# Grouped attention in a gated cross-attention and mixture-of-experts block: TensorE's order changed to one maximum, exponentials, the other maximum, half a chunk's values, with fewer products on constants

## The chip, the cores and the metric

One core of a Trainium2 chip runs the whole program. The time is device microseconds (us) for one execution. The engines are TensorE (PE, with its weight loads PEld), VectorE (DVE), ScalarE (ACT), GpSimd (POOL) and SyncE (SP), which here issues DMAs.

## The reference

```python
q = (Q @ w_q.T).reshape(B, S, G, HG, HD)      # G = 8 groups, HG = 4 heads, HD = 16
k = (K @ w_k.T).reshape(B, S, G, HD)
v = (V @ w_v.T).reshape(B, S, G, HD)
scores = jnp.einsum('bnghd,bmgd->bnghm', q, k) / scale
scores = jnp.where(causal, scores, NEG_INF)
attn = jax.nn.softmax(scores, axis=-1)
out = jnp.einsum('bnghm,bmgd->bnghd', attn, v).reshape(B, S, D)
return out @ w_o.T + b_o
```

Four batches of 512 tokens, width 512. The attention above takes a layernorm of x as its queries; its result, times tanh of a gate, is added to x. A mixture of experts follows (16 experts, 4 per token, and a shared one), again gated and added. The change lies in the attention alone.

## The kernel before

Stages run one after the other: projections of q, k and v to DRAM (`stage_project`), attention (`stage_attend`), output projection and router logits (`stage_close`), routing, experts, combination. `stage_attend` is written by hand for each engine, with semaphores; no scheduler moves anything.

It makes 32 iterations (NIT), one for each batch and group, over 4 heads and 512 x 512 scores. Keys are cut in 4 chunks of 128 (CH). The scores are computed twice. The first time, TensorE multiplies 128 queries by the keys (`max_unit`, L445, into the banks a_mb0 and a_mb1), and VectorE takes the maximum of each row (L413). The maxima are transposed (`turn_maxima`, L451) and put by DMA as one more row beside q. The second time, two iterations later (AHEAD = 2), TensorE computes the transposed scores less their maximum (`exp_unit`, L465, into a_eb), ScalarE takes the exponential into a_at (L392), GpSimd clears the part above the diagonal (L334), and TensorE multiplies by the values (`pv_unit`, L476, into a_pv). ScalarE copies a_pv out once in an iteration (L383).

A chunk `ch` of an iteration has two units `j`, of two heads `t` each. The head t = 0 has its q and k in partitions 0 to 48, t = 1 in partitions 64 to 112, so the two products of a pair use different halves of the array's rows. Chunk `ch` of the exponentials has 512, 384, 256 and 256 columns; the maxima that are computed beside it, for the iteration two later, have 512, 384, 256 and 256 columns too. The values of a chunk have 512, 384, 256 and 128 columns, and four heads stand beside each other in the array's columns.

TensorE's queue in an iteration is, for each chunk: unit j = 0 (exponentials of two heads, maxima of two heads), unit j = 1 (the same), then the values of the chunk before it, all four heads in full width. Waits in this queue:

```python
                    if not isinstance(i, int) or u >= 2:
                        eng.wait_ge(s_rmax, u)
```

is the wait of each maximum u for VectorE to have read the same bank, two maxima before; `exp_unit` waits for ScalarE to have read its bank, a chunk before; `pv_unit` waits for GpSimd (`s_causal`), and at chunk 0 also for ScalarE's copy of a_pv (`s_o`).

Ahead of the exponentials of each unit `spin` issues products of two constant matrices (bf16, 128 x 128, L456) into the bank that the exponentials then overwrite. FILL = (12, 6, 2, 0) is their number in a unit of chunk 0 to 3, so 40 in an iteration; in iteration 0 it is 24 in every unit. Nobody reads their results. Iterations 1 to 29 have maxima beside them, 30 and 31 have none.

Of the kernel before, what the change touches and what calls it, by code (L numbers as in the profile page):

```python
# [16 lines left out]
P = 128  # L17
BATCH, SEQ, D = 4, 512, 512
T = BATCH * SEQ
KD = D // P  # L20
GROUPS, HG, HD = 8, 4, 16
CH = SEQ // P
NIT = BATCH * GROUPS
VW = 2 * HD
HALF = 64
ROW_PAD, ROW_MAX = 3 * HD, 3 * HD + 1
NB = 4
# [241 lines left out]

def stage_attend(nc, io, dram):  # L270

    AHEAD, SPIN, FILL = 2, 96, (12, 6, 2, 0)
    with ExitStack() as c:
        sb = lambda n, s, d=F32: c.enter_context(nc.sbuf_tensor(n, s, d))
        ps = lambda n, s: c.enter_context(nc.psum_tensor(n, s, F32))
# [3 lines left out]
        def sem(name):  # L279
            sems.append(dsem(name))  # L280
            return sems[-1]

        q, k = io["q"], io["k"]
        v = [sb(f"a_v{i}", [P, CH, VW]) for i in range(NB)]
        at = [sb(f"a_at{i}", [P, CH, HG, SEQ]) for i in range(2)]
# [3 lines left out]
        mb = [ps(f"a_mb{i}", [P, SEQ]) for i in range(2)]  # L289
        eb = [ps(f"a_eb{i}", [P, 2, SEQ]) for i in range(2)]  # L290
        pv, mt = ps("a_pv", [P, SEQ]), ps("a_mt", [HG * CH, P])
        s_out = dsem("a_sout")
        s_ld = [dsem(f"a_sld{i}") for i in range(NB)]
        s_smax, s_rmax, s_mt, s_mr = (sem(f"a_s{n}") for n in ("smax", "rmax", "mt", "mr"))
        s_row = [dsem(f"a_srow{i}") for i in range(NB)]
        s_sexp, s_exp, s_causal, s_pv, s_o, s_kept = (sem(f"a_s{n}") for n in ("sexp", "exp", "causal", "pv", "o", "kept"))
# [5 lines left out]
        def steps(eng, body):  # L302

            for r in range(NB):
                body(r, r, 0)
            with eng.Fori(1, NIT // NB - 1) as t:
                for r in range(NB):
                    body(t * NB + r, r, t)
            for r in range(NB):
                body(NIT - NB + r, r, NIT // NB - 1)  # L310

        def after(i, first):

            return not isinstance(i, int) or i >= first

        def exists(i):
            return not isinstance(i, int) or i < NIT

        @block.gpsimd
        def _(eng):  # L320

            due = eng.alloc_register("due7")
            eng.reg_mov(due, NB * 2 * CH + 2)

            def body(i, r, t):
                for ch in range(CH):
                    for hp in range(2):
                        if isinstance(i, int):
                            eng.wait_ge(s_exp, i * 2 * CH + 2 * ch + hp + 2)
                        else:  # L330
                            eng.wait_ge(s_exp, eng.snap(due))
                            eng.reg_add(due, due, 1)
                        square = at[r % 2][:, ch, 2 * hp:2 * hp + 2, ch * P:(ch + 1) * P]
                        eng.affine_select(out=square, in_=square, compare_op=ALU.is_ge, fill=0.0, base=0,  # L334
                                          pattern=[[0, 2], [1, P]], channel_multiplier=-1).then_inc(s_causal, 1)
            steps(eng, body)
# [96 lines left out]

        @block.tensor
        def _(eng):
            def max_unit(i, r, turn, j):

                ch = CH - 1 - turn
                w = max(256, (ch + 1) * P)
                for t in range(2):  # L440
                    u = i * CH * HG + turn * HG + 2 * j + t
                    if not isinstance(i, int) or u >= 2:
                        eng.wait_ge(s_rmax, u)
                    rows = slice(HALF * t, HALF * t + ROW_MAX)
                    eng.matmul(mb[t][:, 0:w], q[r][rows, j, ch * P:(ch + 1) * P], k[r][rows, 0:w], start=True, stop=True).then_inc(s_smax, 1)  # L445

            def turn_maxima(i, r):
                eng.wait_ge(s_rmax, (i + 1) * CH * HG + 1)
                if not isinstance(i, int) or i >= 1:
                    eng.wait_ge(s_mr, i + 1)  # L450
                eng.transpose(mt[:], mx[r % 2][:].rearrange("p h c -> p (h c)"), io["ident"]).then_inc(s_mt, 1)  # L451

            def spin(bank, n):

                for _ in range(n):
                    eng.matmul(bank[:, 0:P], io["onesb"], io["before"], start=True, stop=True)  # L456

            def exp_unit(i, r, ch, j):

                n0 = min(ch * P, 256)  # L460
                eng.wait_ge(s_exp, i * 2 * CH + 2 * ch + j)
                spin(eb[j][:, 0], FILL[ch] if after(i, 1) else 2 * FILL[0])
                for t in range(2):
                    rows = slice(HALF * t, HALF * t + ROW_MAX + 1)
                    mm = eng.matmul(eb[j][:, t, n0:SEQ], k[r][rows, ch * P:(ch + 1) * P], q[r][rows, j, n0:SEQ], start=True, stop=True)  # L465
                mm.then_inc(s_sexp, 1)

            def pv_unit(i, r, ch):

                eng.wait_ge(s_causal, i * 2 * CH + 2 * ch + 3)  # L470
                if ch == 0:
                    eng.wait_ge(s_o, i + 1)
                for j in range(2):
                    for t in range(2):
                        h = head(t, j)
                        mm = eng.matmul(pv[32 * h:32 * h + 32, ch * P:SEQ], v[r][:, ch, :], at[r % 2][:, ch, 2 * j + t, ch * P:SEQ],  # L476
                                        start=ch == 0, stop=ch == CH - 1, skip_group_check=True, tile_position=(0, 32 * h))
                if ch == CH - 1:
                    mm.then_inc(s_pv, 1)

            spin(pv, SPIN)
            for i in range(AHEAD):
                eng.wait_ge(s_ld[i], LD)
                for turn in range(CH):
                    for j in range(2):
                        max_unit(i, i, turn, j)
                        spin(pv, 4 * (CH - turn))
                turn_maxima(i, i)

            def body(i, r, t):  # L490
                eng.wait_ge(s_row[r], ROWS * (t + 1))
                if exists(i + AHEAD):
                    eng.wait_ge(s_ld[(r + AHEAD) % NB], LD * (t + (r + AHEAD) // NB + 1))
                for ch in range(CH):
                    for j in range(2):
                        exp_unit(i, r, ch, j)
                        if exists(i + AHEAD):
                            max_unit(i + AHEAD, (r + AHEAD) % NB, ch, j)
                    if ch:
                        pv_unit(i, r, ch - 1)  # L500
                    elif after(i, 1):
                        pv_unit(i - 1, (r - 1) % NB, CH - 1)
                        if exists(i + 1):
                            turn_maxima(i + 1, r + 1)
            steps(eng, body)
            pv_unit(NIT - 1, NB - 1, CH - 1)


def stage_close(nc, io, dram):
# [927 lines left out]
```

## Time and profile before

| | us |
|---|---|
| runs | 1811.64, 1794.19, 1826.40 |
| median | 1811.64 |
| profiled execution, its own time | 1800.01 |
| its span, first to last instruction | 1798.0 |
| mean granted TensorE clock of the span | 0.858 |
| TensorE matmul busy in the span | 1473.3 (82%) |

[...]

### The profile page before, as it was taken

The page shows a single profiled execution, that of the slowest core. Times are in us where ns is not written, and L with a number is a line of the kernel's source. Part 1 is how long each engine was busy: PE and PEld are TensorE (multiplying, and loading weights), DVE is VectorE, ACT ScalarE, POOL GpSimd, SP SyncE. Part 2 cuts the span into 40 slices and gives each one's busy share as a digit, 9 for nine tenths or more (in the row PEclk, how much of TensorE's full clock was granted, in tenths as well). Part 3 has the DMA queues.
Part 4 walks back from the last instruction along what each step waited for, and adds up shares of the span by engine and source line. Part 5 has one row for each costly group of instructions (what it writes and reads, how often), then busy time and mean ns, then how long its engine had stood idle before and what let it go on. Part 6 is the DMA issues. An engine that isn't in the chain of part 4 may idle for free. (4 is left out here: it accounts for less than half of the span.)

```text
span 1798.0 us, 29246 instructions
## 1 busy us (share of the span) xinstructions
PE 1473.3 (82%) x8596; PEld 1068.5 (59%) x8597; DVE 752.6 (42%) x1939; ACT 537.8 (30%) x951; POOL 610.9 (34%) x810
## 2 busy tenths in 40 slices
PE   6545299999999994856349999999989987799997
PEld 4222265445455452434349999898878976665674
DVE  3111066665555551335860342442443550344353
ACT  2111024444333443011004555454434533100100
POOL 4111012222211221001016777676656774131131
PEclk9778599999776977866559999999989999897997
DMA  5443312232221213544033434434434431342342
GB/s 179 136 124 113 109 34 72 68 79 62 62 62 52 72 48 93 179 185 163 1 120 114 129 130 134 150 130 139 139 112 150 166 122 57 113 134 75 117 140 70
DMA packets 100466, 194.99 MB, mean 108 GB/s; under 512 B 27492, under 2 KB 29028, under 8 KB 99400
## 3 DMA queue, kind: packets, MB, share of 16 engines
q1 hardware_dynamic: 71848, 118.35, 20.6%
q0 software_dynamic: 17200, 55.38, 10.4%
q10 hardware_dynamic: 11376, 20.71, 3.0%
q8 instruction: 24, 0.39, 0.1%
q14 instruction: 18, 0.15, 0.0%
HBM read 130.07 MB, written 64.03 MB: 108 GB/s over the span
## 5 line engine op out<-in xcount | busy, mean ns | idle before, releaser
L413 DVE CUSTOM_DVE_ANT_0 a_mb<-a_mb,late 128x256 f32<-128x256 f32 (+3 forms) x512 | 244.6, 508 | 232.2 <-PE a_mb L445 227.4
L392 ACT ACTIVATE a_at<-a_eb 128x1024 f32<-128x1024 f32 (+3 forms) x256 | 176.9, 703 | 278.8 <-PE a_eb L465 277.2
L334 POOL TENSOR_SCALAR_AFFINE_SELECT a_at<-a_at 128x256 f32<-128x256 f32 x256 | 102.7, 406 | 440.8 <-ACT a_at L392 440.4
L1028 DVE CAST e_w<-e_w 128x480 fp32r<-128x480 f32 x144 | 95.5, 672 | 321.0 <-DMA e_w<-in_w2T 321.0
L1165 PE MATMUL e_gate<-e_w,e_xT 128*128 x948 | 178.8, 340 | 40.0 <-DVE e_w L1036 36.0
L1165 PEld LDWEIGHTS e_gate<-e_w,e_xT 128*128 128x128 f32 x948 | 166.4, 201 | 51.3 <-issue 41.2
L1184 PE MATMUL e_yps<-e_w,e_hT 128*128 x711 | 185.5, 404 | 1.9 <-ACT e_hT L1097 1.4
L1165 PE MATMUL e_up<-e_w,e_xT 128*128 x948 | 174.9, 334 | 0.0
L445 PE MATMUL a_mb<-a_k,a_q 49*128 49x256 f32 (+2 forms) x512 | 149.5, 404 | 22.3 <-DVE a_mx L413 18.0
L1165 PEld LDWEIGHTS e_up<-e_w,e_xT 128*128 128x128 f32 x948 | 154.3, 193 | 0.0
L1184 PEld LDWEIGHTS e_yps<-e_w,e_hT 128*128 128x128 f32 x711 | 128.2, 189 | 27.2 <-issue 1.6
L456 PEld LDWEIGHTS a_eb<-before,onesb 128*128 128x128 bf16 x1432 | 97.3, 108 | 78.2 <-issue 66.0
L456 PE MATMUL a_eb<-before,onesb 128*128 128x128 bf16 x1432 | 131.0, 242 | 0.0
L1032 DVE TENSOR_TENSOR e_w<-e_w 128x480 fp32r<-128x480 f32 x128 | 120.5, 941 | 0.0
L1064 POOL TENSOR_TENSOR e_hT<-e_hc,e_hT 128x384 fp32r<-128x384 f32 x79 | 85.5, 1082 | 102.0 <-ACT e_hc L1098 101.2
L445 PEld LDWEIGHTS a_mb<-a_k,a_q 49*128 49x128 f32 x512 | 79.4, 209 | 66.9 <-DVE a_mx L413 61.3
L1368 PE MATMUL s_yps<-ws,s_h 128*128 128x512 f32 (+1 forms) x288 | 108.3, 515 | 10.9 <-DVE s_h L1319 8.3
L1055 POOL DMA_INDIRECT e_x<-dx,e_idx x79 | 95.1, 1204 | 62.5 <-POOL e_idx L1052 62.5
L465 PE MATMUL a_eb<-a_q,a_k 50*128 50x256 f32 (+2 forms) x512 | 115.8, 455 | 0.0
L1060 POOL TENSOR_TENSOR e_xT<-e_xc,e_xT 128x512 fp32r<-128x512 f32 x79 | 109.3, 1384 | 8.2 <-ACT e_xc L1093 2.4
L476 PE MATMUL a_pv<-a_at,a_v 128*32 128x512 f32 (+3 forms) x1024 | 108.8, 501 | 0.6 <-POOL a_at L334 0.6
L673 PE MATMUL c_op<-c_wo,c_on 128*128 128x512 f32 x128 | 63.5, 659 | 47.8 <-DVE c_on L621 30.0
(194 smaller groups left out, 1873.8 us busy)
## 6 DMA issues: line engine op xcount, KB each, us to landing
e_w<-in_w13T SPq DMA_DIRECT2D x16, 1408.0 KB
dy<-e_y ACTq DMA_DIRECT2D x79, 256.0 KB
dq<-p_parts SPq DMA_DIRECT2D x48, 256.0 KB
a_q<-dq SPq DMA_DIRECT2D x64, 192.0 KB
do<-a_o SPq DMA_DIRECT2D x32, 256.0 KB, 2.2
dx<-c_x POOLq DMA_DIRECT2D x8, 1024.0 KB, 8.2
e_w<-in_w2T SPq DMA_DIRECT2D x16, 512.0 KB
a_k<-dk SPq DMA_DIRECT2D x64, 98.0 KB
```

The costliest lines, as they stand in the source:

```text
L334: eng.affine_select(out=square, in_=square, compare_op=ALU.is_ge, fill=0.0, base=0, pattern=[[0, 2], [1, P]], channel_multiplier=-1).then_ ...
L392: eng.activation(at[r % 2][:, ch, 2 * hp:2 * hp + 2, ch * P:SEQ], eb[hp][:, :, ch * P:SEQ], ACT.Exp, scale=0.25).then_inc(s_exp, 1)
L413: eng.tensor_tensor_reduce(out=mb[t][:, 0:w], in0=mb[t][:, 0:w], in1=io["late"][:, SEQ - w:SEQ], scale=1.0, scalar=3 * NEG, op0=ALU.add, o ...
L445: eng.matmul(mb[t][:, 0:w], q[r][rows, j, ch * P:(ch + 1) * P], k[r][rows, 0:w], start=True, stop=True).then_inc(s_smax, 1)
L456: eng.matmul(bank[:, 0:P], io["onesb"], io["before"], start=True, stop=True)
L465: mm = eng.matmul(eb[j][:, t, n0:SEQ], k[r][rows, ch * P:(ch + 1) * P], q[r][rows, j, n0:SEQ], start=True, stop=True)
L476: mm = eng.matmul(pv[32 * h:32 * h + 32, ch * P:SEQ], v[r][:, ch, :], at[r % 2][:, ch, 2 * j + t, ch * P:SEQ], start=ch == 0, stop=ch == C ...
L1032: eng.tensor_tensor(w[rows, r, 1, cols], w[rows, r, 1, cols].bitcast(F32), w[rows, r, 0, cols].bitcast(F32), ALU.subtract).then_inc(s_low, 1)
L1060: eng.tensor_tensor(xT[r][:, 1], xc[:], xT[r][:, 0].bitcast(F32), ALU.subtract).then_inc(s_xlow, 1)
L1165: mm = eng.matmul(out[r][:], xT[r][:, mine, k, :], w[:, bass.ds(buf, 1), its, at:at + INTER].rearrange("p b n -> p (b n)"), start=not (min ...
L1184: mm = eng.matmul(yps[:], hT[r][0:size, mine, n, :], w[0:size, bass.ds(buf, 1), its, at:at + D].rearrange("p b n -> p (b n)"), start=not ( ...
L1368: mm = eng.matmul(yps[j % 2][:], h[0:size, mine, n, j * P:(j + 1) * P], w2[0:size, its, n, :], start=not (mine or its or n), stop=mine == ...
```

## The change

In `exp_unit` and the table FILL, the products on constants go from (12, 6, 2, 0) to (6, 3, 0, 0) for each unit, 40 to 18 in an iteration. Iteration 0 keeps its 24. `max_unit` issues one head's maximum instead of two. In the loop, head 0's maximum now stands ahead of the unit's constants and exponentials, and head 1's behind them. `pv_unit` makes half of a chunk's columns, for all four heads, and stands behind each unit instead of behind each two, so the first half of a chunk's values is asked for one unit earlier. No DMA, and nothing on the other four engines' queues, is changed.

```diff
-    AHEAD, SPIN, FILL = 2, 96, (12, 6, 2, 0)
+    AHEAD, SPIN, FILL = 2, 96, (6, 3, 0, 0)
...
-            def max_unit(i, r, turn, j):
+            def max_unit(i, r, turn, j, t):
...
-                spin(eb[j][:, 0], FILL[ch] if after(i, 1) else 2 * FILL[0])
+                spin(eb[j][:, 0], FILL[ch] if after(i, 1) else 4 * FILL[0])
...
-            def pv_unit(i, r, ch):
+            def pv_unit(i, r, ch, part):
 
-                eng.wait_ge(s_causal, i * 2 * CH + 2 * ch + 3)
-                if ch == 0:
-                    eng.wait_ge(s_o, i + 1)
+                w = (SEQ - ch * P) // 2
+                cols = slice(ch * P + part * w, ch * P + (part + 1) * w)
+                if part == 0:
+                    eng.wait_ge(s_causal, i * 2 * CH + 2 * ch + 3)
+                    if ch == 0:
+                        eng.wait_ge(s_o, i + 1)
...
                 for ch in range(CH):
                     for j in range(2):
+                        if exists(i + AHEAD):
+                            max_unit(i + AHEAD, (r + AHEAD) % NB, ch, j, 0)
                         exp_unit(i, r, ch, j)
                         if exists(i + AHEAD):
-                            max_unit(i + AHEAD, (r + AHEAD) % NB, ch, j)
-                    if ch:
-                        pv_unit(i, r, ch - 1)
-                    elif after(i, 1):
-                        pv_unit(i - 1, (r - 1) % NB, CH - 1)
-                        if exists(i + 1):
-                            turn_maxima(i + 1, r + 1)
+                            max_unit(i + AHEAD, (r + AHEAD) % NB, ch, j, 1)
+                        if ch:
+                            pv_unit(i, r, ch - 1, j)
+                        elif after(i, 1):
+                            pv_unit(i - 1, (r - 1) % NB, CH - 1, j)
+                            if j == 0 and exists(i + 1):
+                                turn_maxima(i + 1, r + 1)
```

TensorE's queue in iteration 1, chunk 1, unit 1 and chunk 2, unit 0, before (a_mb0 and a_mb1 are the two heads' banks for maxima, a_eb0 and a_eb1 the banks of the two units' exponentials, a_pv the values):

```order
L456 MATMUL a_eb1<-before,onesb 128x128 x6
L465 MATMUL a_eb1<-a_q1,a_k1 128x384 x2
L445 MATMUL a_mb0<-a_k3,a_q3 128x384
L445 MATMUL a_mb1<-a_k3,a_q3 128x384
L476 MATMUL a_pv<-a_at1,a_v1 32x512 x4
L456 MATMUL a_eb0<-before,onesb 128x128 x2
L465 MATMUL a_eb0<-a_q1,a_k1 128x256 x2
L445 MATMUL a_mb0<-a_k3,a_q3 128x256
L445 MATMUL a_mb1<-a_k3,a_q3 128x256
```

The same place in the changed kernel:

```order
L444 MATMUL a_mb0<-a_k3,a_q3 128x384
L455 MATMUL a_eb1<-before,onesb 128x128 x3
L464 MATMUL a_eb1<-a_q1,a_k1 128x384 x2
L444 MATMUL a_mb1<-a_k3,a_q3 128x384
L478 MATMUL a_pv<-a_at1,a_v1 32x256 x4
L444 MATMUL a_mb0<-a_k3,a_q3 128x256
L464 MATMUL a_eb0<-a_q1,a_k1 128x256 x2
L444 MATMUL a_mb1<-a_k3,a_q3 128x256
L478 MATMUL a_pv<-a_at1,a_v1 32x192 x4
```

The two maxima of a pair no longer stand side by side, the six constants are three and the two are gone, and the 512 columns of values are two times 256, with the exponentials of the next unit between.

TensorE's queue at the change of iteration in the changed kernel, from the last unit of iteration 1 to the first of iteration 2:

```order
L444 MATMUL a_mb0<-a_k3,a_q3 128x256
L464 MATMUL a_eb1<-a_q1,a_k1 128x256 x2
L444 MATMUL a_mb1<-a_k3,a_q3 128x256
L478 MATMUL a_pv<-a_at1,a_v1 32x128 x4
L444 MATMUL a_mb0<-a_k0,a_q0 128x512
L455 MATMUL a_eb0<-before,onesb 128x128 x6
L464 MATMUL a_eb0<-a_q2,a_k2 128x512 x2
L444 MATMUL a_mb1<-a_k0,a_q0 128x512
L478 MATMUL a_pv<-a_at1,a_v1 32x64 x4
L450 MATMUL a_mt<-ident,a_mx1 16x128
```

Before, 12 constants stood in each of the two units of chunk 0, with only exponentials and a pair of maxima between them:

```order
L456 MATMUL a_eb0<-before,onesb 128x128 x12
L465 MATMUL a_eb0<-a_q2,a_k2 128x512 x2
L445 MATMUL a_mb0<-a_k0,a_q0 128x512
L445 MATMUL a_mb1<-a_k0,a_q0 128x512
L456 MATMUL a_eb1<-before,onesb 128x128 x12
```

The longest run of constants is 6 now, and a half of the values and a lone maximum lie between two runs.

## Rows read from the trace of the kernel before

**Rows 1.** The page: span, and TensorE's granted clock in 40 slices of the span.
```profile
span 1798.0 us, 29246 instructions
...
PEclk9778599999776977866559999999989999897997
```

**Rows 2.** Windows (stretch, length, busy us and instructions of each engine, clock, DMA): iterations 1 to 29, the tail, one iteration at each clock level.
```profile
core 0: us, PE busy (x) PEld busy (x) DVE busy (x) ACT busy (x) POOL busy (x), PEclk, DMA share, GB/s
...
265.88:680.22 414.34, 392.45 (x3045) 208.21 (x3041) 237.27 (x951) 176.63 (x262) 93.01 (x232) 0.85 0.24 64
680.22:698.00 17.78, 14.39 (x153) 6.95 (x149) 0.28 (x1) 10.81 (x18) 6.06 (x16) 1.00 0.13 46
...
411.04:424.01 12.97, 12.07 (x109) 6.35 (x106) 8.27 (x34) 6.12 (x9) 3.20 (x8) 1.00 0.29 72
...
514.76:532.92 18.16, 17.79 (x110) 9.43 (x107) 8.32 (x34) 6.10 (x10) 3.25 (x8) 0.55 0.19 51
```

**Rows 3.** Waits from 240 to 690 us: total, times, longest.
```profile
PEld a_mb L445 <- DVE a_mx L413: 59.3, 159, 0.7
```

**Rows 4.** Timeline of TensorE's matmuls at clock 1.00: start, length, line, instructions [idle before].
```profile
412.14 0.51 PE L456 MATMUL a_eb<-before,onesb 128*128 128x128 bf16 x6
412.58 0.44 PE L465 MATMUL a_eb<-a_q,a_k 50*128 50x384 f32 x2
...
413.94 1.07 PE L476 MATMUL a_pv<-a_at,a_v 128*32 128x512 f32 x8
414.94 0.28 PE L456 MATMUL a_eb<-before,onesb 128*128 128x128 bf16 x2
...
421.20 0.40 PE L445 MATMUL a_mb<-a_k,a_q 49*128 49x512 f32 x2
421.53 0.84 PE L456 MATMUL a_eb<-before,onesb 128*128 128x128 bf16 x12
422.30 0.50 PE L465 MATMUL a_eb<-a_q,a_k 50*128 50x512 f32 x2
```

**Rows 5.** The same at clock 0.50.
```profile
511.63 1.46 PE L456 MATMUL a_eb<-before,onesb 128*128 128x128 bf16 x12
513.02 0.80 PE L465 MATMUL a_eb<-a_q,a_k 50*128 50x512 f32 x2
513.62 0.63 PE L445 MATMUL a_mb<-a_k,a_q 49*128 49x512 f32 x2
514.18 0.65 PE L476 MATMUL a_pv<-a_at,a_v 128*32 128x128 f32 x8
514.76 0.38 PE L451 MATMUL a_mt<-ident,a_mx 128*16 128x128 f32 x1
...
521.94 0.58 PE L465 MATMUL a_eb<-a_q,a_k 50*128 50x256 f32 x2
...
523.28 1.50 PE L476 MATMUL a_pv<-a_at,a_v 128*32 128x384 f32 x8
524.72 0.58 PE L465 MATMUL a_eb<-a_q,a_k 50*128 50x256 f32 x2
```

**Rows 6.** Timeline of ScalarE and GpSimd behind the exponentials of 422.30 us.
```profile
422.85 1.02 ACT L392 ACTIVATE a_at<-a_eb 128x1024 f32<-128x1024 f32 x1 [0.43 <-PE a_eb L465]
...
424.02 0.41 POOL L334 TENSOR_SCALAR_AFFINE_SELECT a_at<-a_at 128x256 f32<-128x256 f32 x1 [1.04 <-ACT a_at L392]
```

**Rows 7.** Windows ahead of the first fall of the clock: constants alone (L456), then all engines.
```profile
347.38:350.38 3.00, 0.00 (x0) 0.00 (x0) 1.00 0.31 100
...
347.38:350.38 3.00, 2.36 (x19) 1.01 (x19) 2.06 (x11) 1.45 (x4) 1.00 (x3) 1.00 0.31 100
...
640.92:643.92 3.00, 0.00 (x0) 0.00 (x0) 1.00 0.27 93
```

**Rows 8.** The same ahead of rises: constants alone for first and last, then all engines.
```profile
354.20:357.20 3.00, 1.46 (x12) 1.20 (x12) 0.50 0.00 0
...
664.82:667.82 3.00, 1.92 (x18) 1.47 (x15) 0.50 0.00 0
...
354.20:357.20 3.00, 3.00 (x20) 1.79 (x16) 1.41 (x4) 1.33 (x2) 0.41 (x1) 0.50 0.00 0
```

More of the change, by code:

```diff
@@ L435, in _ @@
         def _(eng):
-            def max_unit(i, r, turn, j):
+            def max_unit(i, r, turn, j, t):
                 ch = CH - 1 - turn
                 w = max(256, (ch + 1) * P)
[L440 to L445, printed above, removed]
+                u = i * CH * HG + turn * HG + 2 * j + t
+                if not isinstance(i, int) or u >= 2:
+                    eng.wait_ge(s_rmax, u)
+                rows = slice(HALF * t, HALF * t + ROW_MAX)
+                eng.matmul(mb[t][:, 0:w], q[r][rows, j, ch * P:(ch + 1) * P], k[r][rows, 0:w], start=True, stop=True).then_inc(s_smax, 1)
             def turn_maxima(i, r):
@@ L475, in pv_unit @@
                         h = head(t, j)
-                        mm = eng.matmul(pv[32 * h:32 * h + 32, ch * P:SEQ], v[r][:, ch, :], at[r % 2][:, ch, 2 * j + t, ch * P:SEQ],
-                                        start=ch == 0, stop=ch == CH - 1, skip_group_check=True, tile_position=(0, 32 * h))
-                if ch == CH - 1:
+                        mm = eng.matmul(pv[32 * h:32 * h + 32, cols], v[r][:, ch, :], at[r % 2][:, ch, 2 * j + t, cols],
+                                        start=ch == 0 and part == 0, stop=ch == CH - 1, skip_group_check=True, tile_position=(0, 32 * h))
+                if ch == CH - 1 and part == 1:
                     mm.then_inc(s_pv, 1)
@@ L485, in _ @@
                     for j in range(2):
-                        max_unit(i, i, turn, j)
+                        for t in range(2):
+                            max_unit(i, i, turn, j, t)
                         spin(pv, 4 * (CH - turn))
@@ L495, in body @@
                     for j in range(2):
+                        if exists(i + AHEAD):
+                            max_unit(i + AHEAD, (r + AHEAD) % NB, ch, j, 0)
                         exp_unit(i, r, ch, j)
                         if exists(i + AHEAD):
-                            max_unit(i + AHEAD, (r + AHEAD) % NB, ch, j)
-                    if ch:
-                        pv_unit(i, r, ch - 1)
-                    elif after(i, 1):
-                        pv_unit(i - 1, (r - 1) % NB, CH - 1)
-                        if exists(i + 1):
-                            turn_maxima(i + 1, r + 1)
+                            max_unit(i + AHEAD, (r + AHEAD) % NB, ch, j, 1)
[5 more added lines that the diff above has]
+                                turn_maxima(i + 1, r + 1)
             steps(eng, body)
-            pv_unit(NIT - 1, NB - 1, CH - 1)
+            for part in range(2):
+                pv_unit(NIT - 1, NB - 1, CH - 1, part)
 def stage_close(nc, io, dram):
```

## The prediction

> **What bounds the kernel now.** I read the page, then the attention stage by windows, waits and timeline. Iterations 1 to 29 take 414.34 us, 14.29 each, and TensorE's matmuls are busy 392 of them while VectorE has 237, ScalarE 177 and GpSimd 93 [rows 2]. So TensorE's queue sets the time. Inside it two things matter. First its clock: the page shows digits from 5 to 9 in this stretch [rows 1], and one iteration takes 12.97 us at clock 1.00 and 18.16 us at 0.55 [rows 2]. Second the second pair of maxima in a chunk. TensorE waits there for VectorE to read the banks; over the stage this held the weight loads of the maxima for 59.3 us, 159 times [rows 3]. In the timeline the unit of exponentials at 412.58 (384 columns) is followed by values only at 413.94, 1.36 us later [rows 4].
>
> **Constants removed.** Costs are read from start to start. At clock 1.00, 12 constants take 422.30 - 421.53 = 0.77 us, 6 take 412.58 - 412.14 = 0.44 [rows 4], so one costs 0.055 and a run 0.11 more. An iteration saves two times 6, 3 and 2 products, 22 x 0.055 = 1.21, and two runs vanish (0.22): 1.4 us. At clock 0.50, 12 take 513.02 - 511.63 = 1.39 [rows 5], 0.107 each by the pace of the clock (twice 0.055 less a little overhead), so 22 x 0.107 + 0.2 = 2.6 us.
>
> **Maxima apart.** A pair of two half-height products runs side by side: 512 columns cost 421.53 - 421.20 = 0.33 at clock 1.00 [rows 4] and 514.18 - 513.62 = 0.56 at 0.50 [rows 5], of which 128 columns are 0.055 or 0.107. The trace has no lone maximum that waits for nothing. From below it costs what a pair costs, and from above what it costs now in a second unit; I take the pair. Then 8 units pay one more product each: at clock 1.00 two times (0.33 + 0.27 + 0.22 + 0.22) = 2.1 us, at 0.50 two times (0.56 + 0.45 + 0.35 + 0.35) = 3.4 us. If lone ones overlapped as a pair does, this would be 0.
>
> **Waits that go.** At clock 1.00 a second unit of 384 columns would take 0.28 for exponentials and 0.27 for a pair, 0.56; it takes 1.36, so 0.8 is serial maxima and waiting. The pattern stands in each of four chunks (0.7 to 0.9): 3.2 us. With the exponentials between the two maxima VectorE's reading is covered by them. At 0.50, the unit at 521.94 takes 1.34 until 523.28 against 0.39 + 0.35, 0.6 over, while the 512-column unit takes 513.02 to 514.18, 1.16, which is 0.60 + 0.56 and nothing over [rows 5]; the four chunks, read the same way, give 0, 0.4, 0.6 and 0.8, together 1.8 us.
>
> **Values in halves.** At 0.50, values of 128 columns cost 514.76 - 514.18 = 0.58 and 384 cost 524.72 - 523.28 = 1.44 [rows 5]: 0.43 per 128 columns and 0.15 fixed. Four more fixed parts: 0.6 us. At 1.00, 512 columns cost 1.00 [rows 4], that is 0.86 and 0.14, so 0.6 us too. The range of this term is 0.3 to 1.2. [...]
>
> **New waits.** The first half of a chunk's values is asked for one unit earlier. Its chain: exponentials start at 422.30, ScalarE runs 422.85 to 423.87, GpSimd 424.02 to 424.43 [rows 6], 2.13 us. TensorE's work between, at 1.00: exponentials 0.34 (0.01 over the maxima of 512 columns), maximum 0.33, half values 0.25, maximum 0.27, 3 constants 0.27, exponentials 0.28, maximum 0.27, in all 2.0. So chunk 0 waits 0.1 to 0.2; the same sum for chunks 1 and 2 gives 0.2 to 0.3 each, since ScalarE's share shrinks less than TensorE's. VectorE, with 8.27 us of work an iteration [rows 2], adds some 0.2. Together 0.8 us (0 to 2). At 0.50 TensorE's share doubles and nothing waits.
>
> **One iteration.** At clock 1.00: 12.97 - 1.4 + 2.1 - 3.2 + 0.6 + 0.8 = 11.9 us. At 0.50: 18.16 - 2.6 + 3.4 - 1.8 + 0.6 = 17.8 us. The change is worth about 1.1 us where the clock is full and 0.4 us where it is halved, and a move between the levels is worth 5.9. The clock therefore decides.
>
> **The clock.** From 265 to 680 us the clock falls 11 times and rises 11 times. In the 3 us ahead of all falls no constants run (one lone record in one of them), and TensorE is busy 2.36 of 3.00 us in the first; it is the stretch of chunks 2 and 3 [rows 7]. In the 3 us ahead of each rise, 12 to 20 constants run, and TensorE is busy 3.00 of 3.00, with the 12 in one run from the change of iteration [rows 8]. No rise in this stage stands anywhere else. The change cuts that run to 6 and puts a half of the values and a lone maximum, which feeds 49 of 128 rows, between two runs. It leaves chunks 2 and 3 without a constant, where the falls are. In their favour, the waits there go. The work left in an iteration at 1.00 is: constants 40 to 18, full-height exponentials and values as before, maxima of the same size but one half at a time. [...] I hold that falls come at least as easily, and that what has raised the clock each time is gone. [...]
>
> [...]
>
> **The sum.** Against the profiled execution's own time, 1800.0 (span 1798.0 and 2.0 around it; the median of the runs is 11.6 higher, and I stay with the profiled one). Iterations 1 to 29 at 17.8 are 516 us against 414.3: +102. Two early ones still at full clock: -12. Iteration 0 pays its lone maxima and halves under unchanged constants: +2. Iterations 30 and 31 and the last values, some 15 us at clock 1.00 now [rows 2], at half the clock less their constants: +9. Sum +101, so 1901 us. Other stages are untouched. Own range: 1855 (a few iterations rise again) to 1930 (18.3 us per iteration, and 15 us for the clock's chance elsewhere).
>
> **Rivals.**
> 1. The clock stays up: even spacing removes the thin stretches, and fewer falls need no run of constants to mend. For it: the falls sit where TensorE waited for VectorE, and these waits go. Against it: 11 of 11 rises had a run of 12, and a single fall would not be mended. All iterations at 11.9: 29 x 11.9 = 345 us, -69, iteration 0 +2: 1733; with a few short falls up to 1765. Faster. With a share f of the stage at the low level an iteration takes 11.9 + 5.9 f; that equals the present 14.29 at f = 0.4, so the change wins below that share and loses above it.
> 2. The clock keeps its share, as much low as now (a quarter of the excess, (14.29 - 12.97) / 5.19 = 25%): 11.9 + 0.25 x 5.9 = 13.4, 29 x 0.9 = 26 us less: 1774.
> [...]
>
> **Chances.** Forecast 0.61; rival 1 0.21; rival 2 0.08; rival 3 0.10. A measurement of this kernel tells about 2% from no change. Against the median of 1811.6, faster is below 1775: rival 1 and half of rival 2, 0.25. Same is rival 3 and the other half, 0.14. Slower is 0.61. The range must hold 8 in 10, and the forecast's own is too little; it goes down through rivals 2 and 3 and the upper part of rival 1, to 1760, and up to 1930. The constants' price is firm; the ends of the other unknown terms move an iteration by 1 us, 29 us in all, and are inside.
>
> **What would show it.** Right: PEclk near 5 through the whole attention stretch, no rise after the first iterations, iterations of 17 to 18.5 us, 682 fewer constants in the stage (22 in each of 31 iterations), PEld waits for VectorE gone. The step on the iteration is right if one at clock 1.00 takes 11 to 12.5 us. Wrong: digits of 9 through the stage, a rise ahead of which only 6 constants ran, or an iteration at clock 0.50 that is far from 17.8.

## The result and the profile after

The changed kernel takes 1726.0 us in the median of 4 runs (1717.3 to 1732.5), the kernel before 1802.9 beside it; the ratio is 0.960, with an interval from 0.952 to 0.967. It is faster by 4%. The forecast was 1901 and slower; the first rival, 1733, is what came. The profiled execution took 1732.5 us. Lines of its page:

```profile
span 1730.5 us, 29930 instructions
...
PE 1416.0 (82%) x8938; PEld 1037.9 (60%) x8939; DVE 761.0 (44%) x1939; ACT 538.1 (31%) x951; POOL 607.8 (35%) x810
...
PEclk9878599999999978675599999999999998888898
```

In the stage (slices 6 to 14) every digit is 9, where [rows 1] had 5 to 9: the granted clock was 1.00 from 220 to 626 us of the trace, and did not fall once. In every trace here it stands at 1.00 or at 0.50, with nothing between; other figures are means of a stretch. The windows give iterations 1 to 29 and one of them, to be laid beside [rows 2]:

```profile
core 0: us, PE busy (x) PEld busy (x) DVE busy (x) ACT busy (x) POOL busy (x), PEclk, DMA share, GB/s
266.96:606.03 339.07, 336.01 (x3339) 178.03 (x3333) 250.70 (x955) 176.93 (x262) 94.26 (x232) 1.00 0.30 78
501.43:513.18 11.75, 11.67 (x122) 6.21 (x116) 8.69 (x34) 6.12 (x10) 3.25 (x8) 1.00 0.30 79
```

414.34 us became 339.07, 75.3 less. Half of it, 38 us, is the clock that no longer falls (29 x (14.29 - 12.97)); the other half, 37 us, is the iteration at full clock, 11.69 in the mean against 12.97. The whole profiled execution is 67.5 us shorter: iteration 0 took 0.6 us more (22.5 against 22.0), and what stands before and behind the 30 iterations, nearly all of it untouched, 7.2 more. The waits from 267 to 606 us (who waited for whom, total, times, longest), against [rows 3]:

```profile
PEld a_mb L444 <- DVE a_mx L413: 37.2, 124, 0.4
...
PEld a_pv L478 <- POOL a_at L334: 14.1, 53, 0.3
PEld a_pv L478 <- ACT a_o L383: 2.0, 6, 0.3
```

The waits of the weight loads for VectorE are fewer and shorter, not gone (58.2 us, 155 times, in iterations 1 to 29 before). They cost less than they seem, since loads overlap running products (336.01 and 178.03 us busy within 339.07): TensorE's matmuls were without work for 414.34 - 392.45 = 21.9 us before and for 3.1 now. Waits for GpSimd and ScalarE grew to 16.1 us, 0.6 in an iteration; the kernel before had 2.8 for GpSimd, from 240 to 690 us. In TensorE's timeline below, the four products of `pv_unit` stand as x8 (its 1024 products left 2048 records), and a row costs less in the queue than its length: the six constants are 0.51 us long, and the next row starts 0.44 behind theirs. A unit of chunk 0 and one of chunk 2 (start, length, instructions):

```profile
501.63 0.50 PE L444 MATMUL a_mb<-a_k,a_q 49*128 49x512 f32 x1
502.06 0.51 PE L455 MATMUL a_eb<-before,onesb 128*128 128x128 bf16 x6
502.50 0.51 PE L464 MATMUL a_eb<-a_q,a_k 50*128 50x512 f32 x2
502.85 0.40 PE L444 MATMUL a_mb<-a_k,a_q 49*128 49x512 f32 x1
503.18 0.32 PE L478 MATMUL a_pv<-a_at,a_v 128*32 128x64 f32 x8
...
508.29 0.38 PE L444 MATMUL a_mb<-a_k,a_q 49*128 49x256 f32 x1
508.29 0.49 PE L464 MATMUL a_eb<-a_q,a_k 50*128 50x256 f32 x2
508.52 0.38 PE L444 MATMUL a_mb<-a_k,a_q 49*128 49x256 f32 x1
508.83 0.53 PE L478 MATMUL a_pv<-a_at,a_v 128*32 128x192 f32 x8
```

In this unit of chunk 2 the lone maximum and the exponentials start together, and the second maximum 0.23 us later (in the chunk's other unit, at 507.04, 0.35). In chunk 0, where constants stand between, the first maximum holds the queue 0.43 us by itself (502.06 - 501.63).

### The profile page after: what moved, and what is told of

It reads as the page before. It is cut to its first block and busy times, and to the rows that moved or that the text cites. A ratio compares the mean times of both kernels' runs of the same rounds, so it can differ in the third digit from the quotient of the medians.

```text
span 1730.5 us, 29930 instructions
## 1 busy us (share of the span) xinstructions
PE 1416.0 (82%) x8938; PEld 1037.9 (60%) x8939; DVE 761.0 (44%) x1939; ACT 538.1 (31%) x951; POOL 607.8 (35%) x810
## 3 DMA queue, kind: packets, MB, share of 16 engines
q0 software_dynamic: 17200, 55.38, 10.9%
## 5 line engine op out<-in xcount | busy, mean ns | idle before, releaser
L413 DVE CUSTOM_DVE_ANT_0 a_mb<-a_mb,late 128x256 f32<-128x256 f32 (+3 forms) x512 | 250.9, 503 | 145.4 <-PE a_mb L444 139.4
L1034 DVE CAST e_w<-e_w 128x480 fp32r<-128x480 f32 x144 | 99.6, 701 | 321.3 <-DMA e_w<-in_w2T 321.3
L444 PE MATMUL a_mb<-a_k,a_q 49*128 49x256 f32 (+2 forms) x512 | 190.8, 398 | 0.9
L444 PEld LDWEIGHTS a_mb<-a_k,a_q 49*128 49x128 f32 x512 | 92.2, 184 | 71.6 <-DVE a_mx L413 39.8
L478 PE MATMUL a_pv<-a_at,a_v 128*32 128x256 f32 (+3 forms) x2048 | 122.5, 311 | 6.5 <-POOL a_at L334 2.4
L1070 POOL TENSOR_TENSOR e_hT<-e_hc,e_hT 128x384 fp32r<-128x384 f32 x79 | 89.5, 1133 | 108.7 <-ACT e_hc L1104 108.2
L464 PE MATMUL a_eb<-a_q,a_k 50*128 50x256 f32 (+2 forms) x512 | 120.4, 401 | 0.0
L1038 DVE TENSOR_TENSOR e_w<-e_w 128x480 fp32r<-128x480 f32 x128 | 116.4, 910 | 0.0
L1374 PE MATMUL s_yps<-ws,s_h 128*128 128x512 f32 (+1 forms) x288 | 106.6, 508 | 10.9 <-DVE s_h L1325 8.3
L1374 PEld LDWEIGHTS s_yps<-ws,s_h 128*128 128x128 f32 (+1 forms) x288 | 61.2, 228 | 57.0 <-issue 45.3
L1078 POOL TENSOR_TENSOR e_h<-e_act,e_upc 128x352 f32<-128x352 f32 x79 | 80.5, 1019 | 34.3 <-ACT e_upc L1128 32.0
```

The lines of the kernel that those rows point to most:

```text
L413: eng.tensor_tensor_reduce(out=mb[t][:, 0:w], in0=mb[t][:, 0:w], in1=io["late"][:, SEQ - w:SEQ], scale=1.0, scalar=3 * NEG, op0=ALU.add, o ...
L478: mm = eng.matmul(pv[32 * h:32 * h + 32, cols], v[r][:, ch, :], at[r % 2][:, ch, 2 * j + t, cols], start=ch == 0 and part == 0, stop=ch == ...
L1038: eng.tensor_tensor(w[rows, r, 1, cols], w[rows, r, 1, cols].bitcast(F32), w[rows, r, 0, cols].bitcast(F32), ALU.subtract).then_inc(s_low, 1)
L1374: mm = eng.matmul(yps[j % 2][:], h[0:size, mine, n, j * P:(j + 1) * P], w2[0:size, its, n, :], start=not (mine or its or n), stop=mine == ...
```

## The experiments

The theory after the result (A): the order keeps TensorE evenly at work, so the clock never falls, and the constants are no longer needed to raise it. Against it: the constants are the gain and the clock was luck (B), or some constants are still needed (C).

**Constants alone.** The kernel before in its own order; iteration 0 keeps its 24.

```diff
-    AHEAD, SPIN, FILL = 2, 96, (12, 6, 2, 0)
+    AHEAD, SPIN, FILL = 2, 96, (6, 3, 0, 0)
```

> The kernel before, in its own order, with the constants of the change alone: 6, 3, 0, 0 in a unit instead of 12, 6, 2, 0 (iteration 0 keeps 24). Nothing of the computation changes. Theory A (the order holds the clock: falls come from TensorE's waits for VectorE in chunks 2 and 3, and constants matter little once these waits are gone): these waits are still here and thinner work stands around them, so the clock falls at least as often as in the kernel before and is hardly raised again; iterations near 18.16 - 2.6 = 15.6 us or longer where the clock is low, mean clock of iterations 1 to 29 under 0.8, total 1800 to 1900 us. Theory B (fewer constants are the gain, and the clock held by the luck of its phase in the changed kernel): total 1730 to 1770, iterations of 11.6 us at full clock.

Measured 1847.6 us (1834.8 to 1853.3), ratio 1.028, 1.018 to 1.039. Its iterations 1 to 29:

```profile
267.51:733.50 465.99, 438.05 (x2408) 207.70 (x2404) 237.26 (x951) 175.88 (x261) 93.40 (x232) 0.59 0.21 57
...
449.28:466.67 17.39, 16.53 (x88) 7.80 (x84) 8.28 (x34) 6.12 (x9) 3.26 (x9) 0.50 0.20 53
```

The mean clock is 0.59 against 0.85 [rows 2], iterations at the low level take 17.4 us (15.6 was expected). The clock rose in this stretch five times, for 7 to 34 us each. B falls: the same cut that belongs to a faster kernel makes the old order slower, by 2.8%.

**Order alone.** The changed kernel with (12, 6, 2, 0); iteration 0 keeps its 24.

```diff
-    AHEAD, SPIN, FILL = 2, 96, (6, 3, 0, 0)
+    AHEAD, SPIN, FILL = 2, 96, (12, 6, 2, 0)
```

> The changed kernel with the constants of the kernel before: 12, 6, 2, 0. The order of the change alone. Theory A: the clock never falls in iterations 1 to 29, an iteration is 11.75 + 22 x 0.055 + 0.2, at most 13.1 us, less if part of the constants stands where TensorE waits anyway (12.4); total 1745 to 1770. Theory B: the clock behaves as before, falls some ten times, total 1790 to 1830.

Measured 1773.8 us (1762.4 to 1779.5), ratio 0.988, 0.978 to 0.998; 1.2% is little for this kernel, and the trace says more than the total. The clock is 1.00 through the stage:

```profile
503.26:516.46 13.20, 13.13 (x144) 7.34 (x138) 8.85 (x34) 6.13 (x10) 3.26 (x8) 1.00 0.27 70
```

An iteration of 13.20 us is longer than one of the old order at the same clock (12.97, [rows 2]). With 40 constants the order's whole worth is that all iterations are at that clock. From here the 22 constants are 13.20 - 11.75 = 1.45 us.

**No constants.** The changed kernel with FILL = (0, 0, 0, 0); iteration 0 keeps its 24.

> The changed kernel with no constants at all in iterations 1 to 31 (iteration 0 keeps 24 a unit). Theory A in its strong form (the even order alone keeps the clock): no fall, an iteration loses up to 18 x 0.055 + 4 x 0.11 = 1.4 us, less what new waits for ScalarE and GpSimd take back, so 10.5 to 11.3 us, total 1685 to 1715. Theory C (what my forecast held, only with a lower need: the clock wants some constants): it falls in the first iterations and is not raised again, iterations near 16.5 us, total 1830 to 1880.

Measured 1774.5 us (1771.3 to 1777.0), ratio 0.988, 0.980 to 0.996. Three iterations at clock 1.00 took 29.22 us, 9.7 each, well under the 10.5 expected. At 301.5 us the clock fell and stayed low to the end of the stage, at 13.51 us an iteration:

```profile
269.74:298.96 29.22, 28.63 (x298) 14.15 (x291) 24.57 (x100) 18.11 (x28) 9.79 (x24) 1.00 0.37 97
393.44:406.95 13.51, 13.48 (x101) 6.27 (x97) 8.35 (x34) 6.12 (x10) 3.26 (x8) 0.50 0.26 69
...
298.48:301.48 3.00, 2.73 (x27) 1.18 (x24) 2.78 (x9) 2.29 (x3) 0.57 (x3) 1.00 0.03 5
```

The last row is the 3 us ahead of the fall: TensorE was busy 2.73 of them, with short waits of the weight loads (1.0 us for VectorE, 0.3 for GpSimd, none over 0.4).

So C holds in its first part: without constants this order does not keep the clock. The price of the low level was overestimated (13.5, not 16.5), because the constants cost more than their own length. In this run's timeline of chunk 0 nothing stands between the four products:

```profile
288.31 0.47 PE L444 MATMUL a_mb<-a_k,a_q 49*128 49x512 f32 x1
288.32 0.70 PE L464 MATMUL a_eb<-a_q,a_k 50*128 50x512 f32 x2
288.66 0.40 PE L444 MATMUL a_mb<-a_k,a_q 49*128 49x512 f32 x1
288.99 0.32 PE L478 MATMUL a_pv<-a_at,a_v 128*32 128x64 f32 x8
```

Four products take 0.68 us, as two pairs side by side would. The row of the exponentials is 0.70 us long, where that of two side by side is 0.51 (502.50 us, above): its two products did not run beside each other. In the records of single products, the exponential of head 1, which is second in the queue, starts 0.006 us behind head 0's maximum, and that of head 0 another 0.305 us later. So the maximum of one half of the array ran beside the exponential of the other half, and the remaining exponential beside the second maximum.

**One pause.** The changed kernel, stopped once.

```diff
+        pause = sb("a_pause", [P, 3, 6 * SEQ])
...
             def body(i, r, t):
+                if isinstance(i, int) and i == 3:
+                    for n in range(3):
+                        eng.memset(pause[:, n], 0.0)
                 for ch in range(CH):
```

> The changed kernel with one pause: GpSimd clears 3 x 3072 unused columns at the head of iteration 3, some 9 us, so TensorE stands still once and the clock falls. The pause itself costs about 9 us. My forecast's second step (without a run of 12 constants the clock is not raised again): iterations of 17.8 us from there to the end of the stage, total 1726 + 9 + 27 x 6 = near 1890 us, or as far as it lasts. Its rival (runs of 6 among dense work raise it too): back at full clock within two iterations, total 1740 to 1755.

Measured 1901.8 us, one run. GpSimd's three memsets took 7.9 us together (from 289.36), and TensorE's matmuls stood still for 4.0 us, to 297.99. Within that, at 295.5 us, the clock fell; it came back at 838 us, long behind the stage:

```profile
PEclk9777696555555555568655999999989999898988
...
488.40:506.37 17.97, 17.97 (x118) 8.44 (x116) 8.68 (x34) 6.12 (x9) 3.25 (x8) 0.50 0.19 52
```

The changed kernel has two steady states: 11.75 us an iteration or 17.97. The second is the one forecast. That the totals, 1901.8 and 1901, agree to 1 us is luck: this run holds a pause that the forecast has not, and the sum's terms were off both ways (below). Once low, the clock isn't raised in this stage.

**One pause, more constants.** The order of the change with (12, 6, 2, 0) and the same pause; iteration 0 keeps its 24.

> The order of the change with the constants of the kernel before (12, 6, 2, 0), and the one pause of the run e4_one_pause at the head of iteration 3. It asks what raises the clock: if a run of 12 constants from the change of iteration does it in any order, the clock is back within one or two iterations and the total is near 1774 + 9 + 10 = 1790 us. If the rise needs the old order too (exponentials, a pair and 12 more constants without values between), it stays low: iterations near 17.97 + 22 x 0.107 + 0.2 = 20.5 us, total near 1980 us.

Measured 1999.4 us, one run; 21.54 us an iteration to the end of the stage:

```profile
468.95:490.49 21.54, 21.54 (x142) 11.17 (x138) 8.90 (x34) 6.12 (x10) 3.25 (x8) 0.50 0.16 43
```

A run of 12 constants does not raise the clock in this order. In the kernel before it rose behind such a run within the old order; which part of that order it needs, no run here isolates. At clock 0.50 the 22 constants cost 21.54 - 17.97 = 3.6 us.

**Maxima apart, halves together.** The two halves stand together behind the chunk's second unit, and the transpose of the maxima (`turn_maxima`) behind both, as before the change.

```diff
+                    for part in range(2):
                         if ch:
-                            pv_unit(i, r, ch - 1, j)
+                            pv_unit(i, r, ch - 1, part)
                         elif after(i, 1):
-                            pv_unit(i - 1, (r - 1) % NB, CH - 1, j)
-                            if j == 0 and exists(i + 1):
-                                turn_maxima(i + 1, r + 1)
+                            pv_unit(i - 1, (r - 1) % NB, CH - 1, part)
+                    if not ch and after(i, 1) and exists(i + 1):
+                        turn_maxima(i + 1, r + 1)
```

> The changed kernel, but the two halves of a chunk's values stand together behind the chunk's second unit, as the whole did before. Theory D (the maxima set apart hide VectorE, and that alone keeps the clock): no fall in iterations 1 to 29, iterations near 11.7 us, total 1725 to 1745. Theory E (both parts are needed, since four waits for nothing are followed by a long full stretch only when the values are whole): the clock falls, iterations near 17.5 us from there, total over 1850.

Measured 1880.3 us, one run. The clock fell at 269.9 us, in the first iteration with few constants, and was low for the rest. The timeline before the fall shows two units following each other without values between:

```profile
266.19 0.38 PE L444 MATMUL a_mb<-a_k,a_q 49*128 49x256 f32 x1
...
266.41 0.28 PE L444 MATMUL a_mb<-a_k,a_q 49*128 49x256 f32 x1
267.15 0.38 PE L444 MATMUL a_mb<-a_k,a_q 49*128 49x256 f32 x1 [0.46 <-DVE a_mx L413]
```

The wait for VectorE has only moved from the second maximum to the next unit's first. Theory D falls, on this one run.

**Halves alone.** Maxima as a pair behind the exponentials.

```diff
-                            max_unit(i + AHEAD, (r + AHEAD) % NB, ch, j, 0)
                         exp_unit(i, r, ch, j)
                         if exists(i + AHEAD):
+                            max_unit(i + AHEAD, (r + AHEAD) % NB, ch, j, 0)
                             max_unit(i + AHEAD, (r + AHEAD) % NB, ch, j, 1)
```

> The changed kernel, but the maxima stand as a pair behind the unit's exponentials, as before; only the values are in halves behind each unit. Theory D: the pair's second maximum waits for VectorE less than before, since half of the values stands between two units, yet TensorE stands still in front of the values; the clock falls within some iterations and stays low with runs of 6, iterations near 17.5 us, total 1820 to 1900. If halves alone hold the clock: total 1725 to 1760.

Measured 1763.9 us, one run, between the two expectations.

```profile
264.39:634.28 369.89, 364.25 (x3340) 192.33 (x3333) 242.67 (x957) 179.56 (x262) 94.66 (x232) 0.82 0.27 72
377.41:388.91 11.50, 11.21 (x122) 6.10 (x117) 8.44 (x34) 6.24 (x10) 3.26 (x8) 1.00 0.31 81
```

At full clock its iteration, 11.50 us, is shorter than the changed kernel's 11.75. But the clock held only until 409 us, was low for 85 us (some five iterations), rose once with runs of 6, and fell again. Values between the units are most of what hides VectorE: TensorE's matmuls are without work for 0.3 us of this iteration, 0.9 of one before [rows 2], 0.1 of the changed kernel's. With the maxima set apart as well, the profiles of the changed kernel show no fall. That the maxima are what makes the hold firm isn't shown: this is one run, and the next version has its maxima apart too and fell.

**Constants first.** The changed kernel with the constants of a unit ahead of its first maximum.

```diff
-                eng.wait_ge(s_exp, i * 2 * CH + 2 * ch + j)
-                spin(eb[j][:, 0], FILL[ch] if after(i, 1) else 4 * FILL[0])
...
+                        eng.wait_ge(s_exp, i * 2 * CH + 2 * ch + j)
+                        spin(eb[j][:, 0], FILL[ch] if after(i, 1) else 24)
                         if exists(i + AHEAD):
                             max_unit(i + AHEAD, (r + AHEAD) % NB, ch, j, 0)
                         exp_unit(i, r, ch, j)
```

> The changed kernel with the constants of a unit ahead of head 0's maximum instead of behind it, the same number (6, 3, 0, 0). In the run without constants the first maximum, both exponentials and the second maximum followed each other without a gap (289.64, 289.64 and 290.28 for 512 columns), as if the lone maxima used the half of the array that the exponentials left free. Theory F (a lone maximum beside exponentials is free, and constants between them cost 0.3 us a unit beyond their own time): 4 units x 0.3 = 1.2 us less, iterations of 10.5 to 10.8 us, total 1685 to 1700 if the clock holds. Rival (it costs the same wherever they stand): 11.75 us, total 1726. If the clock falls: 1780 to 1850.

Four runs: 1749.5, 1696.0, 1700.9, 1719.5 us. The one that was profiled is the first:

```profile
266.61:627.44 360.83, 358.95 (x3340) 186.59 (x3334) 241.78 (x957) 176.82 (x262) 94.26 (x232) 0.78 0.27 73
374.64:385.63 10.99, 10.89 (x121) 5.83 (x116) 8.47 (x34) 6.10 (x10) 3.25 (x8) 1.00 0.32 85
```

An iteration takes 10.9 to 11.0 us with the same 18 constants, 0.8 less (1.2 was expected), so their place did cost. The records of iterations 1 to 29 show why: head 1's exponential starts ahead of head 0's, beside the lone maximum, in all 211 units counted here. In the changed kernel it does so in all 116 counted without constants and in none of 117 with them. In this run the clock fell at 470 us, in chunk 3, and stayed low, at 15.35 us an iteration. The run of 1719.5 us has a mean clock of 0.870, against 0.892 and 0.888 in the two faster ones, so it may hold a shorter stretch at the low level. This version is faster where the clock holds, and less firm.

**Where more constants go.** The same with (6, 3, 0, 2), with (8, 4, 0, 0), and the changed kernel again.

> Constants ahead of the first maximum, 6, 3, 0, 2 in a unit. In the run c1_constants_first the clock fell once, at 470 us, out of the stretch of chunks 2 and 3, which has no constants. Theory G (a few constants in that stretch hold the clock): 4 more products and 2 more runs cost at most 0.44 us in an iteration of 10.92, so 11.0 to 11.4, no fall, all runs between 1700 and 1720 us. Rival (the place does not matter): single runs still fall and stand at 1735 or more.

> Constants ahead of the first maximum, 8, 4, 0, 0 in a unit: 6 more products, none of them in chunks 2 and 3. Costs 6 x 0.055 = 0.33 us, an iteration of 11.25. Theory G: the thin stretch is as it was, so some runs still fall; runs from 1705 to 1780 us. Rival (only the number in an iteration counts): no fall, all runs between 1700 and 1720.

> The changed kernel itself, repeated on the same chip. If its order holds the clock by design, no run falls and all lie between 1715 and 1735 us. If the first runs were lucky, some stand at 1760 to 1900, as the one with a pause did (1901.8).

The first measured 1705.1 us (1700.6, 1704.7, 1705.5, 1710.0), ratio 0.955, 0.946 to 0.964. The second 1712.7 (1707.9, 1709.8, 1715.7, 1735.1). The changed kernel again 1729.3 (six runs, 1722.5 to 1733.6), ratio 0.969, 0.962 to 0.976. The first one's iterations:

```profile
268.18:586.58 318.40, 315.76 (x3456) 168.44 (x3450) 241.15 (x957) 176.55 (x262) 94.36 (x232) 1.00 0.32 83
377.56:388.65 11.09, 10.99 (x126) 5.83 (x121) 8.37 (x34) 6.10 (x10) 3.25 (x8) 1.00 0.32 84
```

Four more products in chunk 3 cost 0.1 us, where 0.44 was allowed. No run of this version is over 1710.0 us. It is 24 us (1.4%) under the changed kernel, and its four runs all lie below the six of that one beside it. The profile of (8, 4, 0, 0) shows no fall in iterations 1 to 29 either; its run of 1735.1 us has a mean clock of 0.864, against 0.880 to 0.890 in the others, and where it was low isn't known. With four runs each it isn't shown that this one is the less firm. The changed kernel's ten runs lie within 17 us of each other, with mean clocks of 0.884 to 0.894. An unmended fall costs 6.2 us for each iteration left, so only one in the last two or three could hide there: its hold is no luck.

## Why the prediction was wrong

The step that failed is in the part on the clock: "I hold that falls come at least as easily". They did not come at all. The ground given was the work in the queue: 18 constants instead of 40, the rest as before. I counted what leaves the queue and gave the waits that go too little weight, though I had named the falls' place, chunks 2 and 3 with TensorE busy 2.36 of 3.00 us in the first [rows 7]. Two windows of the changed kernel in these chunks:

```profile
507.07:510.07 3.00, 2.93 (x32) 1.66 (x28) 2.16 (x11) 1.49 (x4) 1.22 (x3) 1.00 0.53 145
508.29:511.29 3.00, 2.99 (x40) 1.84 (x36) 2.08 (x13) 1.30 (x3) 1.22 (x3) 1.00 0.30 99
```

Little of them is idle. Ahead of the fall in the run with the maxima alone apart TensorE was busy 2.42 of 3.00 us, in the run without constants 2.73, in the one with halves alone 2.86. Nor does a fall need a long idle gap: in the kernel before no wait of a maximum's weight load for VectorE was over 0.7 us [rows 3], and the run without constants was busy 28.63 of 29.22 us in its three iterations at clock 1.00. Busy time doesn't tell all, since the run with constants first fell behind a stretch that was busy 2.99 of 3.00:

```profile
467.50:470.50 3.00, 2.99 (x32) 1.67 (x32) 2.39 (x11) 1.46 (x4) 1.22 (x3) 1.00 0.55 150
```

So it is shown that the clock holds by the order together with some constants (constants alone, order alone, no constants), and that this is half of the gain. By what the chip decides to lower the clock stays open.

The other steps, in the prediction's order:

- One iteration at clock 1.00: 11.9 forecast, 11.75 measured (mean of 29: 11.69). At 0.50: 17.8 forecast, 17.97 measured in the run with a pause. This match is luck. The sum starts from 18.16, an iteration at a mean clock of 0.55 [rows 2] and so too short for 0.50. Its term for the constants was 2.6, and 3.6 were measured (21.54 - 17.97). Its other terms were + 3.4 - 1.8 + 0.6 = + 2.2, and from 18.16 to 21.54 it is + 3.4. The errors cancelled.
- Constants removed: 1.4 forecast, 1.45 measured between the run of the order alone and the changed kernel.
- Maxima apart, waits that go, halves, new waits: +2.1 - 3.2 + 0.6 + 0.8 = +0.3 forecast, 13.20 - 12.97 = +0.2 measured. The single terms were less good than their sum. The lower bound, that a lone maximum is free, holds in some units of chunks 2 and 3, and the weight loads' waits for VectorE, which I had taken to go, kept 37.2 of their 58.2 us. Waits for GpSimd and ScalarE were 0.6, without VectorE's share. A half of 256 columns costs 0.57 (505.27 - 504.70), two of them 0.14 more than the 1.00 of the whole, as the term for halves had it. The visits to the values double, from 4 to 8 in an iteration; all changes of form in the queue go from 17 to 24, the transpose left out. What such a change costs beyond the 0.14 of a visit, no run here shows.
- "What has raised the clock each time is gone": right in its effect, as the run with a pause shows, 1901.8 us beside a forecast of 1901. Wrong in its cause: runs of 12 don't raise it in the new order either (1999.4 us). In none of the five profiles with the maxima apart and a fall did the clock rise again within iterations 1 to 29; with the maxima as a pair it did, even with runs of 6 (five times with constants alone, once with halves alone).
- The rivals: the first came with its own sum, 345 us for the 29 iterations, 339.07 measured, and its reason, that the thin stretches go. The objection I held against it, that a single fall would not be mended, was true and did not matter, as no fall came.

## What to carry to other kernels

Ask two questions of a clock that moves, apart: what lets it fall, and what brings it back. This change lost the second and won by the first, so it has two steady states (11.75 and 17.97 us an iteration), and one deliberate pause showed the other (1902 us instead of 1729). Where two orders differ in filled waits, test each part by itself: the same cut of constants was 2.8% slower in the old order and worth some 42 us in the new one (29 x 1.45; the medians are 1773.8 and 1729.3).

## What the runs showed that was not expected

- A lone maximum, two exponentials and a lone maximum follow each other in 0.68 us for 512 columns: as long as two pairs, 0.34 each. The half of the array that one lone product leaves free was used by a product of the other half, and for that the second exponential started ahead of the first, in 227 of 229 units of the run without constants, and in 1 of 211 of the kernel before, where both start together. Constants between them broke this: 18 constants cost 2.0 us an iteration at clock 1.00 (11.75 against 9.7) and 4.5 at 0.50 (17.97 against 13.51), where their own length is 18 x 0.055 = 1.0 and 18 x 0.107 = 1.9 us, and 1.4 at clock 1.00 with the 0.11 of each of 4 runs.
- Half the clock is not twice the time: 17.97 against 11.75 us is 1.53, and 13.51 against 9.7 is 1.39. At the low level the order by itself is not even faster: with the same 18 constants an iteration takes 17.39 us in the old order and 17.97 in the new.
- All 11 falls of the kernel before lay in chunk 3, at its last pair of maxima or the values behind it. Without constants the clock fell at 301.5 us, in the first unit of chunk 1. Why there, no run here tells.
